# Cross-attention of 16 heads: GpSimd multiplies the probabilities by the reciprocals in three parts before they are turned, no reciprocals are turned, and the bias is made in pieces

## The reference

```python
# layer 0: one key and one value head, shared by all 16 query heads
scores = jnp.einsum('bhqd,bkd->bhqk', Q, K) * scale
attn = jax.nn.softmax(scores, axis=-1)
out = jnp.einsum('bhqk,bkd->bhqd', attn, V)

# layer 3: own keys and values for each head, and a bias
rel = jnp.abs(jnp.arange(Nk)[None, :] - jnp.arange(Nq)[:, None] - (Nk - Nq))
bias = -slopes[:, None, None] * rel.astype(jnp.float32)
scores = jnp.einsum('bhqd,bhkd->bhqk', q, k) * scale + bias[None]
attn = jax.nn.softmax(scores, axis=-1)
out = jnp.einsum('bhqk,bhkd->bhqd', attn, v)
```

## Time and profile before

| | us |
|---|---|
| median of three runs | 3329.44 |
| the profiled execution | 3329.15 |
| its span in the profile | 3327.4 |
| busy: PE, DVE, ACT, POOL | 2861.9, 1860.3, 1598.0, 666.5 |
| plain stage, first score to last output | about 304 to 440 |
| biased stage, first score to last output | about 2730 to 2870 |

### The profile page before, as it was taken

The page is one execution under the profiler, slowest core; times in us unless marked ns, Lnnn a source line. Parts: engine busy times, 40 slices in busy tenths (PEclk is TensorE's granted clock), DMA queues, the critical chain, the costliest instruction groups (busy, mean ns, idle before and its releaser), DMA issues. The chain is left out here.

```text
span 3327.4 us, 53684 instructions
## 1 busy us (share of the span) xinstructions
PE 2861.9 (86%) x18568; PEld 1734.6 (52%) x18569; DVE 1860.3 (56%) x4547; ACT 1598.0 (48%) x4375; POOL 666.5 (20%) x741
## 2 busy tenths in 40 slices
PE   7788988759999998779879999999988889859992
PEld 4634653425555554346546544455533456639992
DVE  5645765448788774858566642366423548643333
ACT  5425953127777774841346532165321549613331
POOL 3120020112112110112036520165200003201113
PEclk9879998679999999889989999999999899859996
DMA  1010020200000001000010010000000000141112
GB/s 70 2 19 1 2 84 0 70 0 1 2 2 1 2 13 51 1 13 2 17 40 1 1 63 0 7 1 1 29 0 13 21 8 2 70 169 37 36 35 82
DMA packets 36131, 80.64 MB, mean 24 GB/s; under 512 B 9089, under 2 KB 24530, under 8 KB 32050
## 3 DMA queue, kind: packets, MB, share of 16 engines
q1 hardware_dynamic: 30962, 64.68, 5.4%
q0 software_dynamic: 4368, 11.93, 1.2%
q10 hardware_dynamic: 560, 0.93, 0.1%
HBM read 63.18 MB, written 14.02 MB: 23 GB/s over the span
## 5 line engine op out<-in xcount | busy, mean ns | idle before, releaser
L2471 ACT ACTIVATE scores<-scores,min 128x128 f32<-128x128 f32 (+7 forms) x256 | 198.4, 775 | 86.3 <-DVE min L2454 81.8
L2452 DVE TENSOR_SCALAR zero_marks<-psum 128x128 f32<-128x128 f32 (+7 forms) x256 | 192.1, 750 | 68.1 <-PE psum L2384 66.1
L2454 DVE CUSTOM_DVE_ANT_0 scores<-psum,zero_marks 128x128 f32<-128x128 f32 (+7 forms) x256 | 193.8, 757 | 30.0 <-issue 0.9
L2391 PE MATMUL psum<-ident,scores 128*128 128x128 f32 x1152 | 172.9, 277 | 16.6 <-ACT probsT L2488 13.5
L2488 ACT ACTIVATE probsT<-psum 128x128 f32<-128x128 f32 (+7 forms) x256 | 163.2, 637 | 32.3 <-PE psum L2391 31.3
L3903 PE MATMUL psum<-Hn,W 128*128 128x512 f32 x384 | 169.4, 604 | 8.6 <-PEq L419 8.6
L1609 ACT ACTIVATE XT<-psum,b_of_tile 128x128 f32<-128x128 f32 x312 | 89.2, 369 | 178.3 <-PE psum L1529 178.3
L1529 PE MATMUL psum<-x_gatheredT,XT 128*128 128x128 f32 x1248 | 153.0, 283 | 6.1 <-issue 3.1
L1529 PEld LDWEIGHTS psum<-x_gatheredT,XT 128*128 128x128 f32 x1248 | 148.1, 198 | 13.0 <-issue 11.8
L2391 PEld LDWEIGHTS psum<-ident,scores 128*128 128x128 f32 x1152 | 123.3, 141 | 56.1 <-issue 30.2
L3761 POOL TENSOR_TENSOR probs<-probs,stat 128x512 f32<-128x512 f32 (+1 forms) x128 | 123.4, 988 | 101.3 <-DVE stat L3725 98.9
(11 more groups left out here) (634 smaller groups left out, 6764.7 us busy)
## 6 DMA issues: line engine op xcount, KB each, us to landing
W<-in_L3f_W SPq DMA_DIRECT2D x16, 1024.0 KB, 22.3
L3f_y_rows<-y SPq DMA_DIRECT2D x39, 128.0 KB, 1.7
early_weights<-in_L2f_Wqkv SPq DMA_DIRECT2D x2, 1536.0 KB
W<-in_L2f_W SPq DMA_DIRECT2D x2, 1536.0 KB
XT<-in_xT SPq DMA_DIRECT2D x1, 2048.0 KB, 9.3
Xtok<-in_xtok SPq DMA_DIRECT2D x1, 2048.0 KB
L0f_rows<-Xtok SPq DMA_DIRECT2D x4, 512.0 KB, 2.9
W<-in_L0f_W SPq DMA_DIRECT2D x2, 1024.0 KB
```

Source lines behind the costliest of these rows:

```text
L2391: ins = pe.transpose(turned[:, kt * P:(kt + 1) * P], Sc[:, i % ROT, kt * P:(kt + 1) * P], K.ident[:])
L2452: dve.tensor_scalar(zero[:, i % 2, 0:n], sc(i)[:, 0:n], 0.0, -NEG, ALU.is_equal, ALU.mult)
L2454: dve.tensor_tensor_reduce(Sc[:, i % ROT, 0:n], sc(i)[:, 0:n], zero[:, i % 2, 0:n], 1.0, -NEG, ALU.add, ALU.min, low[:, i % ROT:i % ROT + ...
L2471: act.activation(p, p, ACT.Exp, bias=low[:, i % ROT:i % ROT + 1], scale=-1.0, accum_out=sums[:, u % 2, h:h + 1]).then_inc(s["exp_done"], 1)
```

## The change

GpSimd now multiplies the probabilities by the reciprocals in place, before PE turns them, in three instructions of a step: heads 0 to 3, heads 4 to 6, head 7 (`PARTS`). PE's `turn(n, g)` waits for the part instead of for the exponentials. The spread, the turning and the copy of the reciprocals are gone (L737, L775, L841), and `output` is a plain copy. The eight reciprocals of a step are made in three instructions, each behind its part of the exponentials. DVE's queue is written in another order, and `output` lags by three steps instead of two. The bias of a pair of steps is made in two instructions of four heads, one in each step of the pair before, behind that step's multiplications.

```diff
                 @block.gpsimd
-                    def bias(m):
+                    def bias(m, piece):
                         if m >= 2:
                             pool.wait_ge(s["min_done"], 3 * B * (m - 1))
                         tt, c, _ = order[B * m]
-                        pool.tensor_tensor(bias_of[:, m % 2], middle(alibi[0][:, tt, :], HPC), inner(alibi[1][:, c * HPC:(c + 1) * HPC], CTX), ALU.mult).then_inc(s["biased"], 1)
+                        own = HPC // B
+                        pool.tensor_tensor(bias_of[:, m % 2, piece * own:(piece + 1) * own], middle(alibi[0][:, tt, :], own),
+                                           inner(alibi[1][:, c * HPC + piece * own:c * HPC + (piece + 1) * own], CTX), ALU.mult).then_inc(s["biased"], 1)
 
                     for n in range(steps):
-                        if alibi and n % B == 0 and n // B + 1 < steps // B:
-                            bias(n // B + 1)
-                        pool.wait_ge(s["recip_done"], n + 1)
-                        if n >= 2:
-                            pool.wait_ge(s["recip_turned"], n - 1)
-                        pool.tensor_copy(Rx[:, n % 2, :].rearrange("p (h d) -> p h d", h=HPC), inner(st(n, 2), HD)).then_inc(s["recip_spread"], 1)
+                        for i, heads in enumerate(PARTS):
+                            pool.wait_ge(s["recip_done"], 3 * n + i + 1)
+                            v = probs(n)[:, heads.start * CTX:heads.stop * CTX].rearrange("p (h k) -> p h k", k=CTX)
+                            pool.tensor_tensor(v, v, inner(st(n, 2)[:, heads], CTX), ALU.mult).then_inc(s["normed"], 1)
+                        if alibi and n // B + 1 < steps // B:
+                            bias(n // B + 1, n % B)
 
                 @block.tensor
                     def turn(n, g):
-                        pe.wait_ge(s["exp_done"], 3 * n + g + 1)
+                        pe.wait_ge(s["normed"], 3 * n + g + 1)
...
                         last.then_inc(s["pv_done"], 1)
-                        pe.wait_ge(s["recip_spread"], n + 1)
-                        pe.transpose(K.bank[6 + n % 2][:, P:2 * P], Rx[:, n % 2, :], K.ident[:]).then_inc(s["recip_turned"], 1)
 
                 @block.vector
                             if g == 0:
-                                dve.wait_ge(s["biased"], n // B + 1)
+                                dve.wait_ge(s["biased"], B * (n // B + 1))
...
                     def output(n):
                         dve.wait_ge(s["pv_done"], n + 1)
-                        dve.wait_ge(s["recip_out"], n + 1)
-                        dve.tensor_tensor(OT[:, order[n][1], token(n):token(n) + P], K.bank[6 + n % 2][:, 0:P], RT[:, n % 2, :], ALU.mult).then_inc(s["out"], 1)
-
-                    for g in (0, 2, 1):
-                        minima(0, g)
+                        dve.tensor_copy(OT[:, order[n][1], token(n):token(n) + P], K.bank[6 + n % 2][:, 0:P]).then_inc(s["out"], 1)
+
+                    def recip(n, i):
+                        dve.wait_ge(s["exp_done"], 3 * n + i + 1)
+                        if n >= 2:
+                            dve.wait_ge(s["normed"], 3 * (n - 2) + i + 1)
+                        own = PARTS[i]
+                        dve.reciprocal(st(n, 2)[:, own], st(n, 1)[:, own]).then_inc(s["recip_done"], 1)
+
                     for n in range(steps):
-                        if n + 1 < steps:
-                            for g in (0, 2, 1):
-                                minima(n + 1, g)
-                        if n >= 2:
-                            dve.wait_ge(s["pv_done"], n - 1)
-                        probs_out(n, 0)
-                        probs_out(n, 2)
-                        dve.wait_ge(s["exp_done"], 3 * n + 3)
-                        if n >= 2:
-                            dve.wait_ge(s["recip_spread"], n - 1)
-                        dve.reciprocal(st(n, 2), st(n, 1)).then_inc(s["recip_done"], 1)
-                        if n >= 2:
-                            output(n - 2)
+                        for g in (0, 2, 1):
+                            minima(n, g)
+                        if n >= 1:
+                            if n >= 3:
+                                dve.wait_ge(s["pv_done"], n - 2)
+                            probs_out(n - 1, 0)
+                        recip(n, 0)
+                        if n >= 1:
+                            probs_out(n - 1, 2)
+                        recip(n, 1)
+                        recip(n, 2)
+                        if n >= 3:
+                            output(n - 3)
...
                 @block.scalar
                     for n in range(steps):
...
-                            act.wait_ge(s["recip_done"], n - 1)
+                            act.wait_ge(s["recip_done"], 3 * (n - 1))
...
-                            if h == 3 and n >= 2:
-                                recip_out(n - 2)
```

More of the change, by code:

```diff
@@ L706, in cross_attention @@
             stat = sbuf(inside, nc, "stat", [P, 2, 3, HPC])
-            Rx = sbuf(inside, nc, "recip_spread", [P, 2, P])
-            RT = sbuf(inside, nc, "recipT", [P, 2, P])
             if alibi:
@@ L711, in cross_attention @@
                 arrive(nc, K)
-            names = "biased recip_spread recip_turned scored min_done exp_done recip_done turned probs_out probs_out_act recip_out pv_done out"
+            names = "biased scored min_done exp_done recip_done normed turned probs_out probs_out_act pv_done out"
             with phase(nc, K.sems, names) as (block, s):
@@ L719, in cross_attention @@
                 st = lambda n, i: stat[:, n % 2, i, :]
+                PARTS = (slice(0, 4), slice(4, 7), slice(7, 8))
                 @block.gpsimd
                 def _(pool):
-                    def bias(m):
+                    def bias(m, piece):
                         if m >= 2:
@@ L726, in bias @@
                         tt, c, _ = order[B * m]
-                        pool.tensor_tensor(bias_of[:, m % 2], middle(alibi[0][:, tt, :], HPC), inner(alibi[1][:, c * HPC:(c + 1) * HPC], CTX), ALU.mult).then_inc(s["biased"], 1)
+                        own = HPC // B
+                        pool.tensor_tensor(bias_of[:, m % 2, piece * own:(piece + 1) * own], middle(alibi[0][:, tt, :], own),
+                                           inner(alibi[1][:, c * HPC + piece * own:c * HPC + (piece + 1) * own], CTX), ALU.mult).then_inc(s["biased"], 1)
                     if alibi:
-                        bias(0)
+                        for piece in range(B):
+                            bias(0, piece)
                     for n in range(steps):
-                        if alibi and n % B == 0 and n // B + 1 < steps // B:
-                            bias(n // B + 1)
-                        pool.wait_ge(s["recip_done"], n + 1)
-                        if n >= 2:
-                            pool.wait_ge(s["recip_turned"], n - 1)
-                        pool.tensor_copy(Rx[:, n % 2, :].rearrange("p (h d) -> p h d", h=HPC), inner(st(n, 2), HD)).then_inc(s["recip_spread"], 1)
+                        for i, heads in enumerate(PARTS):
[4 more added lines that the diff above has]
+                            bias(n // B + 1, n % B)
                 @block.tensor
@@ L832, in _ @@
-                    output(steps - 2)
-                    output(steps - 1)
+                        dve.tensor_copy(OT[:, order[n][1], token(n):token(n) + P], K.bank[6 + n % 2][:, 0:P]).then_inc(s["out"], 1)
[5 more added lines that the diff above has]
+                        dve.reciprocal(st(n, 2)[:, own], st(n, 1)[:, own]).then_inc(s["recip_done"], 1)
@@ L835, in _ @@
+                    if steps >= 3:
+                        dve.wait_ge(s["pv_done"], steps - 2)
+                    probs_out(steps - 1, 0)
+                    probs_out(steps - 1, 2)
+                    for n in range(steps - 3, steps):
+                        output(n)
                 @block.scalar
                 def _(act):
[L837 to L841, removed]
@@ L864, in _ @@
                                 probs_out(n - 1)
-                            if h == 3 and n >= 2:
-                                recip_out(n - 2)
                     probs_out(steps - 1)
-                    recip_out(steps - 2)
-                    recip_out(steps - 1)
         finish(nc, K, lambda k, t: Wo[:, k, :], tile_of_block(OT), DC, bias=bo[:])
```

## The result

| | before | after |
|---|---|---|
| median (runs) | 3328.35 us (4) | 3405.87 us (4) |
| lowest to highest | 3324.01 to 3330.47 | 3403.15 to 3409.78 |
| profiled execution | 3329.15 | 3405.94 |
| its span | 3327.4 | 3404.2 |
| plain stage, first to last head 0 | 128.34 | 142.17 |

The ratio is 1.0236 (95%: 1.0223 to 1.0249), so the kernel is slower by 77 us, against a forecast of 73 for the profiled execution. The last three rows are made from one trace each. They take the start of ACT's exponential of head 0 in the first and in the last of a stage's 32 steps. The plain stage lost 13.8 us, the biased stage 63.3, and the other ten parts nothing.

The account below looks back on a forecast made before the run. PE was taken to bind at 4.19 us a step, ACT close behind. Plain stage +12 and biased stage +61 make +73 us on the profiled 3329.15: forecast 3402 us, own range 3390 to 3415, wider range 3385 to 3430.

Parts of the forecast that it names:

- The bound before, and the saving of PE: Both stages: PE binds at 4.19 us a step; one transpose less saves 0.26, leaving 3.93, but hidden, worth nothing.
- The plain step: Plain stage, ACT-DVE chain: 3.54 to the last sum plus 1.02 gap, 4.56 us against 4.19; +12 us in 32 steps.
- The short biased step: Biased stage, same ACT-DVE chain with its own lengths: 5.05 us, +0.86 against 4.19, in 17 of 32 steps.
- The long biased step: Biased stage, DVE's minimum waits for the half bias behind GpSimd's multiplications: 7.28 us, +3.09, in 15 of 32 steps.
- GpSimd's rate: GpSimd's multiplications: 1.67 ns an element and 0.185 fixed, so parts of 1.22, 0.96 and 0.44 us.
- rival 1: Both stages: DVE slows all GpSimd work by 1.22; +13 us in long steps, +5 plain, about 3420; chance 0.10.
- row of 1.272: GpSimd row of 512 elements, 1.22 times as long as another of 1.042; read as support for slowing by DVE.
- The wait that GpSimd adds ahead of PE's turns: Plain stage: multiplications delay PE's turns, but PE has 0.63 us of slack a step, so it costs nothing.
- rival 2: Biased stage: PE's clock falls and PE binds, 1.1 us more per affected step; +18 to +35 us, 3420 to 3437; chance 0.12.
- Rival 3: Biased stage: GpSimd finishes the bias before it is wanted, all steps short; +40 us, 3369; chance 0.05.
- Rival 4: Both stages: ACT's gap between steps is small enough to hide, PE's 3.93 binds; faster, 3312 us; chance 0.03.

Follow-up runs that it names:

- The second experiment: Kernel after, with DVE's output copy moved from behind the last reciprocal to ahead of the reciprocals: 3395.25 us, ratio 1.0207 to the kernel before.
- The first experiment: Kernel after, with GpSimd issuing each half bias ahead of its step's multiplications instead of behind them: 3363.84 us, ratio 1.0121 to the kernel before.
- The fourth experiment: Kernel after, with GpSimd's multiplications cut to 8 of each head's 154 keys, all waits kept: 3393.74 us, ratio 1.0205 to the kernel before.
- The fifth: Kernel after, with half bias ahead of multiplications, first minima ahead of last reciprocal, multiplications cut to 8 keys: 3333.67 us, ratio 1.0016 to the kernel before.

## Why the prediction was right

**The bound before, and the saving of PE.** That PE's 0.26 us a step would be hidden held: no run here had steps of 3.93. With the chain between ACT and DVE shortened the plain stage came back to the time of before (4.17 a step), and only without most of GpSimd's work to 4.05.

**The plain step.** Forecast 4.56, measured 4.61 in 28 of 31 steps. The terms, forecast then measured: last sum read 3.54, 3.57; to the reciprocal 0.03, 0.03; to the copy 0.11, 0.08; the copy 0.20, 0.19; minimum and start of ACT 0.68, 0.75. The last is the one that was too small. The minimum itself takes its 0.64, but ACT starts 0.11 behind its end instead of 0.04. I had taken 0.04 from the first step of the stage. The earlier trace rows held the better figure: before, a minimum ended at 2794.98 and the next head 0 was due 4.19 after 2790.90, at 2795.09, which is 0.11. The trace shows what the first step lacks. In the kernel after, in the first two steps of each stage, head 0's exponential carries the one wait, for the minimum, and starts 0.04 behind it. That holds in the second step too, where ACT had worked and then waited 0.77 and 0.99 us, much as in later steps. From the third step on, where the code has two more waits (`turned`, `recip_done`), a semaphore instruction of its own stands in ACT's queue ahead of the exponential. It starts 0.03 behind the minimum's end, and the exponential 0.08 to 0.09 behind that, in the kernels before and after alike. Per stage of 31 intervals the forecast makes 11.5 us. The measured 13.8 adds 28 x (4.614 - 4.187 - 0.37) = 1.6 and 0.8 in the first three intervals, which took 3.22, 3.67 and 4.21 before and 4.10, 4.44 and 4.44 after. The second experiment confirms the chain by 0.19 for 0.19.

**The short biased step.** 5.05 forecast, 5.05 measured, but as 3.87 + 0.08 + 0.19 + 0.91: the reciprocal started 0.03 earlier, the copy's terms came out 0.04 smaller, and minima and start of ACT 0.07 longer. That these cancel is luck.

**The long biased step.** Forecast 7.28, measured 7.35. GpSimd's start 2.50, 2.51; end of the half bias 6.34, 6.26; to DVE 0.10, 0.17; minima and start 0.84, 0.92. Here too a part cancels, 0.08 of 0.15. The first experiment took the half bias off the chain alone.

**GpSimd's rate.** The parts took 1.21, 0.96 and 0.44, so rival 1 (a factor of 1.22) is out. This is what the Trainium skill (SBUF — State Buffer, Who interferes with whom) says of VectorE instructions with at most one SBUF input: the means of L737 lie on the linear rate of the earlier trace rows beside a DVE that reads PSUM. The Trainium skill's cycle count for a two-input operation (GPSIMD Engine Reference, Elementwise — side-by-side cycle accounting) would have made an estimated 1.4 us of 616 elements at 2.2 ns; the trace has 1.21. But the prediction read its row of 1.272 wrongly. These rows of the kernel before stand behind it:

```profile
L3632 POOL TENSOR_TENSOR straight<-straight,norm 128x512 f32<-128x512 f32 x64 | 66.8, 1044 | 22.6 <-DVE norm L3623 20.4
...
L220 POOL TENSOR_TENSOR Xtok<-Xtok,early_weights 128x256 f32<-128x256 f32 x48 | 33.0, 731 | 36.5 <-POOLq L54 34.3 <-SPq L54 2.2
```

The row of 1.272 (L3629) is an addition of two full inputs, L3632 a multiplication by one value for each head (a spread operand), on the same buffer in the same stage. No VectorE instruction of that stage has two SBUF inputs, so by the Trainium skill's rule on the port, as the prediction cites it, the port is not what makes the 1.22, and all 64 of L3629 take 1.26 to 1.28. From the 0.731 of 256 elements with two full inputs (L220) to 1.272 of 512 it is 2.1 ns an element, close to the 2.2 above. So 1.67 ns goes with the spread operand and 2.1 with two full ones; no run changed the operand alone, so this is a reading of rows. The forecast chose the right row for the new multiplications. The wait that GpSimd adds ahead of PE's turns was costed at nothing in the plain stage, for 0.63 us of slack. The fourth experiment shows that: 4.60 with and without the work. The fifth adds the condition: when the step gets down to 4.17, the cover is used up and the work costs 0.12.

**PE's clock.** Here rival 2 was right that the clock falls, and the forecast was right that this costs next to nothing. I had kept the clock out of the sum. It did fall: 0.87 in the biased stage. Two stretches of the kernel after, with the columns of the earlier trace rows:

```profile
2867.00:2873.00 6.00, 4.77 (x62) 2.61 (x54) 2.83 (x18) 2.50 (x13) 3.75 (x4) 1.00 0.01 3
2874.00:2880.00 6.00, 5.68 (x18) 3.42 (x18) 3.91 (x23) 4.24 (x19) 3.75 (x4) 0.50 0.00 0
```

The second is at the lower level, 1.2 GHz. But rival 2 priced each such step at 1.1 us for PE binding, and PE does not bind in a step of 7.35 with 3.93 us of work: its slower matmuls can mostly fall into time in which ACT waits anyway. Eleven of the 15 long steps hold time at the lower level. In nine of them it is at most 1.8 us, and all of these but one (7.47) took 7.35. Only two long steps took 8.01, those with 2.9 and 3.0 us of it: 2 x 0.66 = 1.3 us in all, not 18. The 63.3 us of the biased stage are then 15 x 3.09 + 16 x 0.86 = 60.1 as forecast, 15 x 0.07 = 1.1 for the long steps' 7.35, 1.3 for the clock, 0.4 in a long step of 7.47 and a short one of 5.33 (the first experiment has this one too, at full clock, so it isn't the clock's), and 0.4 in the first three intervals.

**Rival 3**, a bias that is in time, is out by the wait of 2.20. The experiment that moved the half bias makes its case by hand: it forecast 3369, and the ratio of that kernel, 1.0121, makes 3369 of the 3328. **Rival 4**, faster, would have needed a gap of under 0.65; the gap is 4.61 - 3.57 = 1.04.

## What to carry to other kernels

- When a wait is moved in an in-order queue, write down what now stands behind it and who waits for that. Here the reciprocals of a step were on no one's path before; moved ahead of the next step's minima they coupled two engines, and the step became the sum of both engines' parts (3.57 + 1.05, about 4.6 us), where PE alone had set it before (4.19). In such a loop every piece counts: taking a 0.19 us copy out gave 0.19, and putting the minima ahead of the last reciprocal gave 0.44, until the next limit.
- A producer's instruction for a later step belongs ahead of the waits of the present one. The same half bias, issued 2.6 us of work earlier, gave back 38 us.
- Take the start latency of an engine from a steady step, not from the first of a stage: 0.11 against 0.04 us here, from the third step of each stage on. The first steps lack waits that the code makes only for later ones.

## What the hardware showed that was not expected

- PE's granted clock fell in short stretches and came back, again and again, in the biased stage of the kernel after. The stretches that I looked at had PE waiting up to 2.9 us (for DVE's `probsT` copies) in every second step just before. In the first experiment, with PE busy 86% of the same stage and waits for DVE of at most 0.8 us in the stretch shown, it stayed at 1.00. The short multiplications show the price best: a long step of 6.58 takes about 7.24 where it holds a stretch at the lower level, so 0.66 of the 0.77 us gained in that step is lost again.
- Two more waits ahead of an exponential put a semaphore instruction of its own into ACT's queue, and the start behind a minimum went from 0.04 to 0.11 or 0.12 us (kernel after, from the third step of both stages on).
- GpSimd's multiplication with a spread operand keeps its line far down: 0.185 us and 1.67 ns an element, from 1024 elements, give 0.24 for 32 elements, and 0.24 was measured.
- A copy of 128 x 128 from PSUM by DVE lasts 0.27 us, but the next instruction starts 0.19 behind its start. The second number is the one that a chain pays.
